# A state-space block on one core: the decay exponents from bf16 differences, clamped by VectorE, and a reordered last context tile

## The reference

```python
zxbcdt = _rms(x, norm_w) @ in_proj_w
z, xBC = zxbcdt[..., :512], zxbcdt[..., 512:1280]
dt = softplus(zxbcdt[..., -8:] + dt_bias)              # 8 heads
xBC = silu(conv_b + sum(padded[:, k:k + L] * conv_w[:, k] for k in range(4)))
xh, Bm, Cm = xBC[..., :512], xBC[..., 512:640], xBC[..., 640:]
decay, dbx = exp(dt * -exp(A_log)), dt[..., None] * xh
def step(h, inp):                                      # over the 512 rows
    h = h * dec[:, :, None, None] + u[..., None] * bt[:, None, None, :]
    return h, einsum('bhpn,bn->bhp', h, ct)            # h: 8 heads x 64 x 128
y = ys + D_skip * xh
return x + _rms(y * silu(z), gnorm_w) @ out_proj_w
```

## Time and profile before

| | |
|---|---|
| median of 3 runs | 1530.23 us (1529.27 to 1531.14) |
| the profiled execution's own time | 1529.02 us |
| its span, first to last instruction | 1527.4 us, 35942 instructions |
| granted TensorE clock, mean | 0.965 |
| busy: PE / PEld / DVE / ACT / POOL | 89% / 66% / 69% / 70% / 6% |
| chain that ended last | PE 62%, DVE 13%, ACT 13%, issue 10% |

### The profile page before, as it was taken

The page is one execution under the profiler, slowest core; times in us unless marked ns, Lnnn a source line. Parts: engine busy times, 40 slices in busy tenths (PEclk is TensorE's granted clock), DMA queues, the critical chain, the costliest instruction groups (busy, mean ns, idle before and its releaser), DMA issues.

```text
span 1527.4 us, 35942 instructions
## 1 busy us (share of the span) xinstructions
PE 1355.9 (89%) x13426; PEld 1007.1 (66%) x13426; DVE 1053.9 (69%) x2343; ACT 1065.7 (70%) x3209; POOL 97.1 (6%) x151
## 2 busy tenths in 40 slices
PE   7899899998998889999888999988889999788855
PEld 6788566666666556777666667766666777566644
DVE  4766667766788778677777767877776787777400
ACT  4566567756778887777887677787876777887422
POOL 2100122220000000000000000000000000000000
PEclk9999999999999999999999999999999999999855
DMA  8232310003131112122011112200121121010100
GB/s 294 74 97 97 115 44 1 1 1 125 47 96 41 56 57 84 38 68 64 29 57 57 57 57 57 84 29 29 57 84 42 43 84 57 29 38 20 42 1 14
DMA packets 69883, 90.42 MB, mean 59 GB/s; under 512 B 5520, under 2 KB 58896, under 8 KB 69328
## 3 DMA queue, kind: packets, MB, share of 16 engines
q1 hardware_dynamic: 69600, 87.87, 18.2%
q0 software_dynamic: 112, 0.26, 0.1%
HBM read 71.33 MB, written 16.78 MB: 58 GB/s over the span
## 4 chain that ended last, share of the span: by engine, by line
PE 62%; DVE 13%; ACT 13%; issue 10%; POOL 0%; DMA 0%; ACTq 0%; DVEq 0%; SPq 0%; POOLq 0%
PE ps L1251 13%; PE ps L1593 11%; PE ps L1258 8%; PE ps L1265 7%; PE ps L1622 6%; ACT arena L755 5%; DVE arena L1200 5%; PE ps L1667 3%; PE ps L1328 2%; PE ps L1420 2%; PE ps L1437 2%; PE ps L1576 2%; ACT R L815 1%; PE ps L1393 1%; DVE arena L914 1%
## 5 line engine op out<-in xcount | busy, mean ns | idle before, releaser
L1251 PE MATMUL ps<-W,arena 128*128 128x128 f32 x2896 | 429.4, 282 | 22.3 <-ACT arena L755 19.8
L755 ACT ACTIVATE arena<-ps,nmax 128x512 f32<-128x512 f32 x640 | 435.1, 686 | 0.4 <-issue 0.2
L1251 PEld LDWEIGHTS ps<-W,arena 128*128 128x128 f32 x2896 | 320.8, 144 | 170.4 <-issue 128.4
L762 ACT COPY arena<-ps 128x512 f32<-128x512 f32 x320 | 187.2, 585 | 209.7 <-PE ps L1251 205.6
L1180 DVE TENSOR_REDUCE nmax<-ps 128x1 f32<-128x512 f32 x320 | 206.1, 686 | 118.8 <-PE ps L1593 80.9
L1200 DVE COPY arena<-ps 128x512 f32<-128x512 f32 x320 | 213.7, 686 | 24.9 <-PE ps L1251 14.5
L1593 PE MATMUL ps<-W,arena 32*128 32x512 f32 x1280 | 184.4, 643 | 36.5 <-DVE arena L1200 35.1
L1622 PE MATMUL ps<-arena 128*32 128x128 f32 x5120 | 173.8, 277 | 31.8 <-ACT arena L762 31.6
L1183 DVE TENSOR_REDUCE nmax<-ps 128x2 f32<-128x1024 f32 x160 | 193.7, 1211 | 0.0
L1622 PEld LDWEIGHTS ps<-arena 128*32 128x32 f32 x5120 | 130.7, 110 | 69.7 <-ACT arena L762 59.2
L755 ACT ACTIVATION_READ_ACCUMULATOR arena<-ps,nmax 128x1 f32 x640 | 131.1, 205 | 0.0
(11 more groups left out here) (221 smaller groups left out, 1702.0 us busy)
## 6 DMA issues: line engine op xcount, KB each, us to landing
W<-keys SPq DMA_DIRECT2D x48, 512.0 KB, 3.7
arena<-values SPq DMA_DIRECT2D x48, 512.0 KB, 5.3
keys<-W SPq DMA_DIRECT2D x16, 448.0 KB, 3.3
values<-W SPq DMA_DIRECT2D x16, 448.0 KB, 3.9
W<-keys SPq DMA_DIRECT2D x16, 256.0 KB, 2.8
arena<-values SPq DMA_DIRECT2D x16, 256.0 KB, 3.3
W<-in_pack SPq DMA_DIRECT2D x1, 3180.0 KB, 10.4
CX<-in_ctx SPq DMA_DIRECT2D x4, 512.0 KB, 11.1
```

The lines of the kernel that those rows point to most:

```text
L755: nc.scalar.activation(Pr[:, a, :], ps[:, a, :], ACT.Exp, bias=nmax[:, u % 32:u % 32 + 1], accum_out=den[:, u % 32:u % 32 + 1]).then_inc(s ...
L762: nc.scalar.copy(PT[:, (4 * Q + a) % 8, :, :].rearrange("p k n -> p (k n)"), psT).then_inc(sem("u_ev_act"), 1)
L1251: ins = nc.tensor.transpose(dst[:, k * P:(k + 1) * P], src[:, k * P:(k + 1) * P], ident)
```

## The change

**How the exponents are made.** The sums of dA up to each row are taken once for all 16 tiles (`decay_sums`), split into three bf16 parts (`decay_parts`), laid beside rows of ones and of -1, and turned by 16 bf16 transposes (`decay_turns`) into `cs_i` and `cs_j`. A tile's exponents are then a bf16 product over 64 partitions of `cs_i` with `dAm`, which GpSimd spreads over the heads with a mask `head8`, for two tiles at a time (`head_rows`). Above the diagonal the differences are positive, so VectorE holds them at or under zero on the way from PSUM to `seg` (a `min` over 128 x 1024), and ScalarE's Exp reads and writes `seg` in SBUF.

**Chunk 0.** No inter product, no scaling of it, no decay of the state and no zeroing; the state is a copy of the product.

**The last context tile.** `softplus` moves from tile 15 to tile 14 on VectorE; TensorE makes both items of tile 15 ahead of its keys; the second convolution of tile 15 stands in front of VectorE's last values instead of behind them. The three small fp32 products that made `dec` stand inside tile k = 0, and their Exp behind the tile's own.

Parts of the diff that the text speaks of (`m_soft` and `m_exp` are renamed `m_steps` and `m_steps_act`, counts of `m_y` and `m_z` are tables since chunk 0 has fewer):

```diff
 # GpSimd
-            def masked_dA(k):
-                nc.gpsimd.tensor_tensor(dAm[:, :, :], w("tri_le").unsqueeze(1).to_broadcast([P, HM, P]),
-                                        wide(dts[:, 11, k, :], P), ALU.mult).then_inc(sem("m_dAm"), 1)
+            def head_rows(m):
+                nc.gpsimd.tensor_tensor(dAm[:, m % 2, :, :], cs_j[:, m, :].unsqueeze(1).to_broadcast([P, HM, P]),
+                                        wide(w("head8"), P), ALU.mult).then_inc(sem("m_dAm"), 1)
...
             for k in range(NT):
-                if k + 1 < NT:
+                if k % 2 and k + 3 < NT:
                     pool.wait_ge(sem("m_rows"), 2 * k + 1)
-                    masked_dA(k + 1)
+                    head_rows((k + 3) // 2)
 # ScalarE
+                def intra_weights():
+                    act.wait_ge(sem("m_M"), 2 * k + 1)
+                    nc.scalar.activation(r.seg[:, :, :], r.seg[:, :, :], ACT.Exp).then_inc(sem("m_E"), 1)
+
                 if k < NT:
-                    act.wait_ge(sem("m_rows"), 2 * k + 1)
-                    if k >= 2:
-                        act.wait_ge(sem("m_intra"), k - 1)
-                    for i in range(2):
-                        ins = nc.scalar.activation(r.seg[:, 4 * i:4 * i + 4, :].rearrange("p g n -> p (g n)"), X[1 + i], ACT.Exp)
-                    ins.then_inc(sem("m_E"), 1)
+                    if k:
+                        intra_weights()
                     act.wait_ge(sem("m_rows"), 2 * k + 2)
 # VectorE, context stage
                 if k == NT - 2:
-                    softplus_front()
+                    softplus_series()
+                    softplus()
                 if k == NT - 1:
-                    softplus()
+                    decay_parts()
+                    ctx_keys(k)
+                    decay_rows()
                 conv(k, 0)
+                if k == NT - 1:
+                    conv(k, 1)
...
-            conv(NT - 1, 1)
 # VectorE, Mamba stage
                 if k < NT:
+                    dve.wait_ge(sem("m_rows"), 2 * k + 1)
+                    if k >= 2:
+                        dve.wait_ge(sem("m_intra"), k - 1)
+                    nc.vector.tensor_scalar(r.seg, ps[:, 4 * (k % 2) + 1:4 * (k % 2) + 3, :].rearrange("p i (h n) -> p (i h) n", n=P),
+                                            0.0, None, ALU.min).then_inc(sem("m_M"), 1)
                     dve.wait_ge(sem("m_xr"), k + 1)
+                    dve.wait_ge(sem("m_E"), k + 1)
                     nc.vector.tensor_tensor(r.BG[:, 1, :], X[0][:, P:2 * P], w("tri_le"), ALU.mult).then_inc(sem("m_cb"), 1)
...
-                    if k < FT:
-                        dve.wait_ge(sem("m_Hd"), k + 1)
+                    if c == 0:
+                        dve.wait_ge(sem("m_state"), k + 1)
+                        nc.vector.tensor_copy(Hst[:, b, :], X[3]).then_inc(sem("m_H"), 1)
+                    elif k < FT:
+                        dve.wait_ge(sem("m_Hd"), k - NB + 1)
 # TensorE
                     for i in range(2):
-                        ins = mm(X[1 + i], w("tri_gt"), dAm[:, 4 * i:4 * i + 4, :].rearrange("p h n -> p (h n)"),
+                        ins = mm(X[1 + i], cs_i[rows, m, :], dAm[rows, m % 2, 4 * i:4 * i + 4, :].rearrange("p h n -> p (h n)"),
                                  start=True, stop=True)
...
                 if k < NT:
-                    pe.wait_ge(sem("m_E"), k + 1)
                     if c:
+                        pe.wait_ge(sem("m_E"), k + 1)
                         pe.wait_ge(sem("m_H"), k - NB + 1)
-                    mm(X[1], xs[:, 5, part], Hst[:, b, :], start=True, stop=True).then_inc(sem("m_z"), 1)
+                        mm(X[1], xs[:, 5, part], Hst[:, b, :], start=True, stop=True).then_inc(sem("m_z"), 1)
```

More of the change, by code:

```diff
@@ L22 @@
 FT = (NCH - 1) * NB
+Z_AT = [2 * k - min(k, NB) for k in range(NT + 1)]
+Y_AT = [4 * k - 2 * min(k, NB) for k in range(NT + 1)]
 FIRST_AT = {NT - 2: (0, 1), NT - 1: (2, 3)}
@@ L310, in build @@
         ident = w("ident")
+        cs_T = [ps[:, n, :].bitcast(BF16).rearrange("p (m n) -> p m n", m=NT // 2) for n in (0, 1, 2)]
         side = [[ps[:, 3 * s + i, :] for i in range(3)] for s in range(2)]
@@ L582, in _ @@
                 ctx_values(k)
[L583 to L588, removed]
             silu(NT - 1, 0)
             silu(NT - 1, 1)
+            nc.scalar.activation(warm[:, :], col("bk3", 0), ACT.Exp)
             def first_xT(b):
@@ new lines, in decay_parts @@
+            def decay_parts():
+                cs = side[0][0][:, 0:NT * HM].rearrange("p (k h) -> p k h", k=NT)
+                part = lambda i: cs_parts[:, 0, :, HM * i:HM * i + HM]
+                nc.vector.tensor_copy(ident_b, ident)
+                dve.wait_ge(sem("m_cs"), 1)
+                dve.wait_ge(sem("zeroed"), 4)
+                nc.vector.tensor_copy(part(0), cs).then_inc(sem("m_steps"), 1)
+                dve.wait_ge(sem("m_steps"), 20)
+                nc.vector.tensor_tensor(d(9), cs, part(0), ALU.subtract).then_inc(sem("m_steps"), 1)
+                dve.wait_ge(sem("m_steps"), 21)
+                nc.vector.tensor_copy(part(1), d(9)).then_inc(sem("m_steps"), 1)
+                dve.wait_ge(sem("m_steps"), 22)
+                nc.vector.tensor_tensor(part(2), d(9), part(1), ALU.subtract).then_inc(sem("m_steps"), 1)
@@ L1337, in time_steps, with decay_sums, decay_turns @@
                 ins.then_inc(sem("m_dt0"), 1)
+            def decay_sums():
+                pe.wait_ge(sem("c_act"), NT - 1)
+                pe.wait_ge(sem("m_steps"), 19)
+                mm(side[0][0][:, 0:NT * HM], w("tri_le"), dts[:, 11, :, :].rearrange("p a h -> p (a h)"), start=True,
+                   stop=True).then_inc(sem("m_cs"), 1)
+            def decay_turns():
+                pe.wait_ge(sem("m_steps_act"), 4)
+                pe.wait_ge(sem("c_dve"), NT - 1)
+                for v in (1, 0):
+                    for m in range(NT // 2):
+                        ins = nc.tensor.transpose(cs_T[2 if v and m == 0 else v][:, m, :],
+                                                  cs_parts[:, v, 2 * m:2 * m + 2, :].rearrange("p k n -> p (k n)"), ident_b)
+                        if v and m == 0:
+                            ins.then_inc(sem("m_cs"), 1)
+                    ins.then_inc(sem("m_cs"), 1)
             ctx_turn(0)
```

190 lines of the change are left out of this document (122 added, 68 removed).

## The result

| | before | after |
|---|---|---|
| median | 1529.83 us (1529.27 to 1531.14, 4 runs) | 1560.33 us (1557.81 to 1561.88, 4 runs) |
| the profiled execution, its span | 1529.02 us, 1527.4 us | 1561.46 us, 1559.9 us |
| granted TensorE clock, mean | 0.965 | 0.947 |
| busy: PE / PEld / DVE / ACT / POOL | 89% / 66% / 69% / 70% / 6% | 87% / 65% / 68% / 68% / 5% |
| chain that ended last | PE 62%, DVE 13%, ACT 13%, issue 10% | PE 59%, DVE 15%, ACT 14%, issue 11% |

The change made the kernel slower: ratio 1.0198, 95% interval 1.0183 to 1.0213, that is + 30.5 us. Forecast A had said 1557.

What follows compares the result with a forecast made beforehand. TensorE was taken as the bound before, its gain lost to a wait for clamp and Exp: Mamba stage + 16.8, head - 5.0, clock + 15 to 17, about + 27 on 1530.2, so 1557 us (1547 to 1569; 8 of 10: 1539 to 1569).

Steps and rivals of the forecast that it cites:

- Forecast A: Whole kernel: slower by the new wait with clock falls, about + 27 us, 1557 us (1547 to 1569); chance 0.62.
- head, to the end of tile 1: Before the row tiles: convolutions end earlier, at 183.2, and z starts earlier; - 5.0 us, from - 9 to - 3.
- tiles 2, 3 and 4: Mamba stage: z waits for rows copied behind Exp, tiles 1 to 3 some + 0.3 together; tile 4 + 0.6.
- tiles 5 to 12: Mamba stage: inter product waits for clamp and Exp, tile 11.45 us against 10.11; 8 x 1.34 = 10.7 us.
- tile 8, `late_weights`: Row tile 8 has `late_weights` in front of its clamp: + 0.5 us.
- tiles 13 and 14: Chunk 3: inter product starts at I + 3.85 instead of I + 3.3; + 0.5 each, 1.0 us.
- tile 15: Last row tile: both `first_rows`, the second waiting for GpSimd, stand before the clamp; inter product later, + 3.7 us.
- clock, tiles 2 to 15: TensorE's clock falls behind the new idle time in two tiles out of three, 10 x 1.7; + 15 to 17 us.
- Rival B: Whole kernel: same new wait but the clock holds; + 11.8, 1542 us (1539 to 1546); chance 0.26.
- C: Row tiles: TensorE stays the bound, clamped exponents ready by I + 2.55; faster, 1508 us; chance 0.03.
- D: Row tiles and head: even, clamp at 0.74 and Exp at 0.9 us, head at - 9; 1529 us; chance 0.04.
- E: Row tiles: the clock falls for long in every tile; + 28 + 11.8, 1570 us; chance 0.05.

Runs made afterwards that it cites:

- the kernel with the filled gap: Changed kernel plus two unused fp32 products of 512 columns on TensorE before the inter product of tiles 1 to 15; 1542.34 us, ratio 1.0099.
- the early kernel: Changed kernel with the exponents, VectorE's clamp and ScalarE's Exp made a tile ahead; 1512.79 us, ratio 0.9909.
- the last kernel: Exponents a tile ahead, plus GpSimd's product waiting for VectorE's `seg`, sum of squares behind next tile's copies, inter product before the turn; 1505.97 us, ratio 0.9848.
- the clamp in the middle: Changed kernel with only the clamp moved on VectorE, behind the gated rows and before the state's decay and update; 1530.16 us, ratio 1.0008.

## Why the prediction was right, step by step

The forecast was + 27 us over the median; + 30.5 came. The mechanism was the one forecast; that the total came so near is in part luck, since the share of the wait less the head's gain was 1.7 us smaller than forecast and that of the clock larger. The sum in the trace, by the same stretches:

| step | forecast | measured | from |
|---|---|---|---|
| head, to the end of tile 1 | - 5.0 | - 3.2 | 190.79 - 195.89, and 12.92 - 11.03 in tile 1 |
| tiles 2, 3 and 4 | + 0.9 | + 1.2 | 0.31 twice, 0.59 |
| tiles 5 to 12 | + 10.7 | + 10.6 | 8 x (11.42 - 10.10) |
| tile 8, `late_weights` | + 0.5 | + 0.4 | 11.85 - 11.42 |
| tiles 13 and 14 | + 1.0 | + 1.0 | 10.55 - 10.05, 10.53 - 10.04 |
| tile 15 | + 3.7 | + 3.7 | inter product at I + 6.96 against I + 3.3 |
| clock, tiles 2 to 15 | + 15 to 17 | + 17.5 | 6 x 1.70, 2.85, 3.00, 1.5 |
| last sum of the stage | + 27 to 29 | + 31.1 | 382.55 - 351.43 |

The tiles without the clock's share are read from the kernel with the filled gap, of which each length agrees with the undisturbed tiles of the changed one. The span grew by 32.5: 1.4 more lie in the attention stage, whose instructions are the same. The prediction had its length unchanged. TensorE was busy there for 1029.6 us instead of 1027.1 with as many products, at a mean clock of 0.95 instead of 0.96, so this too goes with the clock; why it fell in other places there stays open.

**The chain.** It holds at each link. The clamp starts at I + 2.74 (forecast 2.76), Exp at I + 4.00, the inter product at I + 5.11 (5.18), the tile lasts 11.42 us (11.45). The clamp takes 1.22 us, the value taken from the reduction with as many elements; Exp from SBUF 1.06 (1.09). The two bf16 products show as 0.55 us in a chain of waits, where I took 0.43; it only shortened TensorE's idle time, 2.3 us where I had 2.6. That `head_rows` is hidden in the wait for Exp held as well, as the early kernel showed when that cover went; and the clamp was not held up by it, as the prediction had assumed (1.22 us from 239.56 on, with the product of GpSimd running from 240.03).

**The clock.** Right in kind and nearly in size. I forecast ten falls in 15 tiles. In tiles 2 to 15 nine came, 17.5 us; with the low clock of the head in tile 0 and tile 1, some 3.5 us more than in the kernel with the filled gap, the clock's share is about 21 us of the 31.1. A fall costs 1.70 us in chunks 0 to 2, as worked out from z at either level. In tiles 13 and 14 it costs 2.9, since it starts before the inter product and takes that and the turn in too (2.07 and 0.85 us, at the full clock 1.13 and some 0.4). The filled gap shows for tiles 2 to 14 that the clock falls with the idle time. Rival B's 1542 us and the 1542.34 of that kernel agree by chance: by the ratio it is 1545, and its last sum is 11.8 us late with 1.7 of the clock in it, where B had 11.8 without any.

The Trainium skill ("TensorE: Matmul & The Clock Gate", HAM oscillation — how this bites in real kernels) tells of a kernel that waits some 3 to 5 us in front of every inner tile and starts each at the low clock. The prediction took from it that every tile would pay, though the wait here is shorter. It doesn't hold for this one: tiles 5, 7 and 11 kept the clock with the same 2.3 us of idle time, tile 2 with 2.2 and tile 4 with 1.5.

**The head.** The mis-sized step, with two errors in it. The convolutions ended at 180.7 and not at 183.2: the reordering alone is worth 7.3 us, as its own run showed, where I gave the whole head 5.0. Against that I let the lower clock end with z of tile 0. It lasted to 200 us and through z of tile 1 (3.64 us instead of 1.98 in the timeline), for 2.5 us. In the kernel with the filled gap it ended by 190 and the head came to - 6.7.

**Row tile 15.** The price of the wait was right to 0.1 us. The 5.15 us by which the tile grew hold 1.5 of the clock besides.

**The rivals.** B fell with the first low stretch in chunk 1; what it described, the wait without the clock, comes to 10.1 us. C's condition, clamped exponents by I + 2.55, was not met by this change but can be: the last kernel meets it and its tile of 8.89 us is nearly the 8.82 that I gave for TensorE as the bound. D fell with the clamp's 1.22 us. E's fall in every tile didn't come. The rival that the clamp costs by its length wherever it stands falls with the clamp a tile early, where TensorE is busy without a gap; in the middle of the tail 0.55 us a tile were left of it.

## What to carry to other kernels

When an instruction is put between two engines that met directly, price the queue it is put in: here 1.22 us of `min` with 2.7 us in front of it cost 1.8 us a tile against the same program without it, 0.55 when it stood 1.3 us earlier, and made TensorE wait no more when it stood a tile ahead. An idle time of TensorE that is new in a dense loop is paid twice when its clock falls, and useless products put into it show the second share in a single run, if it is read tile by tile. When a wait is taken away, look for what it had covered: the next two kept the tiles at 9.95 and 9.13 us, and only with them gone did the cheaper products pay in full.

## What the runs showed of the hardware

VectorE's product of two SBUF operands, 1.22 us alone, took 2.93 when it began 0.05 us behind a 1.90 us product of GpSimd: it ended 1.08 us behind it. In the kernel without the clamp it began 1.09 us behind such a product, took 1.89 and again ended 1.08 behind it. So it looks held until the product is through, rather than slowed. The clamp, from PSUM, ran beside the same product at 1.22, and the product kept its 1.90. The hold goes both ways; in the last kernel a GpSimd instruction of one column took 1.10 us beside VectorE's product, and 0.19 otherwise:
```profile
246.13 1.23 DVE L1109 TENSOR_TENSOR arena<-arena,BG 128x1024 f32<-128x1024 f32 x1
246.30 1.10 POOL L450 TENSOR_SCALAR stm<-stm 128x1 f32<-128x1 f32 x1 [6.83 <-ACT W L637]
...
255.20 0.19 POOL L450 TENSOR_SCALAR stm<-stm 128x1 f32<-128x1 f32 x1 [2.39 <-ACT arena L637]
```

TensorE kept 2.4 GHz through chunks 1 and 2 with 0.5 us of idle time in tiles of 9.60 us (no clamp) and 1.05 in 10.15 (the clamp in the middle), and lost it in nine of fourteen tiles with mostly 2.3 in 11.42. In chunk 3 it kept it with 0.76 in 10.05 (the kernel before); 1.8 in 10.03 (no clamp) went with a fall in one of two tiles. The same idle time kept the clock in one tile and lost it in the next, and the falls came at the same tiles in two executions; what decides between them no run here shows. Once low, it stayed low for 16.6 us at the head with TensorE busy for 15.82 of them, for some 3.4 us in tile 6 and some 6.9 in tile 13 (worked out from the mean clock of the stretches shown).
